# Expert rows in a fused attention and mixture-of-experts kernel: normed rows stored once and fetched by a list of row numbers

## The chip, the cores and the metric

The kernel runs as one program on the 8 cores of one Trainium2 chip. The metric is the device time in microseconds (us) of the slowest core. Cores exchange nothing; each computes 2048 of the 16384 rows of the output.

## The reference

```python
x = x + attn(layernorm(x))        # x: (2, 8192, 1024) f32
x = x + ffn(layernorm(x))

# attn: q, k, v = split(x @ W + b); softmax(q k^T / 32, causal) @ v
# ffn, for each row x of its input:
logits = x @ router_w             # 8 experts
topw, topi = top_k(softmax(logits), 2)
routed = sum over the 2 chosen experts e of topw * (silu(x @ w1[e]) @ w2[e])
gate, up = split(x @ shared_gate_up)
shared = sigmoid(x @ shared_gate_w) * ((silu(gate) * up) @ shared_down)
return routed + shared
```

## The kernel before, in words

A core owns 16 tiles of 128 rows (`NT = 16`) and works through the causal attention of its batch in 8 blocks of 1024 keys (`NKB = 8`). A unit is a pair (key block kb, row tile t); 72 units run in the order of the list `units`. Per unit TensorE (PE) makes the scores (`qk`, L542), VectorE (DVE) the row maximum, ScalarE (ACT) the exponentials `P` (L572), a transposing DMA on SP's queue turns them into `PT` (L589), and PE multiplies by the normed rows of the block (`av`, L605). The keys' rows are loaded on POOL's queue (L69), normed into `XN` on ACT (L277) and turned into `XT` by transposing DMAs on SP's queue (L287). Scores wait for all of `XT` that they read, `av` waits for `PT`.

When a tile has seen its last block it is retired in four steps that are laid between the units: `retire_a` and `retire_b` finish the attention and norm the row into `xf` (two buffers), `retire_c` makes the router's decision, `retire_d` (L739) counts each row's place in its two experts. Every expert has 640 places (`CAP = 640`), place numbers lie in `posu`. Two indirect DMAs on POOL's queue (L761) then write each row of `xf`, 2 KB in bf16, into the two places of the DRAM tensor `G`. So that places that no row takes hold zeros, 16 DMAs (L840, x = 2 to 17 of the unit loop) write zeros over the first 5120 rows of `G`, 640 KB each; they sit on POOL's queue among the loads of `xkv` rows and, from x = 10, the 8 pieces of the value weights `WV` (L845).

After attention come the shared expert's first product (`gate_up`, L790) and then the 8 experts. An expert's 640 rows are one DMA `xn<-G` (`load_rows`, L914) on SP's queue; PE turns them with the identity (`turn_rows`, L921), 8 transposes for each of 5 groups of 128 rows. Expert 0 is loaded and turned under `gate_up`. In the expert loop (L1079) expert ex does its first product (L1089, 128 matmuls of 320 columns), then its second (L1114, 5 groups s of 16 matmuls), and the turning of expert ex+1's groups lies between these groups, for s = 0 to 3. At s = 3, when expert ex+1's rows have left `xn`, the rows of expert ex+2 are loaded. `Y<-ys` (L1129, on SP's queue) stores each group of 128 result rows, 512 KB in f32, from three buffers `ys`. The weights come on POOL's queue in 8 pieces each, cast from f32 to bf16 on the way: `w1` of expert ex+2 after the first product of ex, `w2` of ex+2 after the second. Six tiles of the attention's result were parked in DRAM and come back (`O<-R`, L949, on SP's queue) after expert 0's first product.

At the end POOL gathers result rows from `Y` by `lohi`, the lower and the higher place of each row (L1150), DVE adds them (L1158), and PE's last product (L1174) adds the shared expert.

SP's and POOL's queues are in order: an instruction that waits holds back all that stand behind it. Two queues of transfers result, one for what SP issues and one for what POOL issues; both are served by the same 16 DMA engines.

Of the kernel before, what the change touches and what calls it, by code (L numbers as in the profile page):

```python
# [81 lines left out]
def build_program():  # L82
    nc = bass.Bass("TRN2", target_bir_lowering=False)

    def dram(name, shape, dty=F32, kind="ExternalInput"):
        return nc.dram_tensor(name, shape, dty, kind=kind).ap()
# [16 lines left out]
    G = dram("G", [7 * CAP + 2048, D], BF16, kind="Internal")  # L103
# [6 lines left out]
    def at(name, cols, dty, off):  # L110
        return nc.alloc_sbuf_tensor_at(name, [128, cols], dty, offset=base + off)
# [12 lines left out]
    zero = at("zero", 1024, BF16, 188416)  # L124
# [33 lines left out]
    bb_bf = at("bb_bf", 8, BF16, small_at[0] - 32)  # L158
    bqk_bf = small("bqk_bf", 16, BF16)
# [226 lines left out]
    k_tri = SP.dma(lambda e: e.dma_start(out=tri[:], in_=trih), d_tri)  # L386

# [351 lines left out]
    def retire_d(t):  # L739

        i = t % 2
        n = ring_n[0] % 3
        ring_n[0] += 1
        PE.wait(ohb_ready[t], ring_free[n], k_tri, k_ones)
        PE.quiet(lambda e: e.matmul(ring[n][:, 0:8], tri[:], ohb[i][:], start=True, stop=True))
        k = PE.do(lambda e: e.matmul(ring[n][:, 8:16], ones[:], ohb[i][:], start=True, stop=True))
        ohb_free[i] = k
        a = DVE.do(lambda e: e.tensor_tensor(out=rk[:], in0=ring[n][:, 0:8], in1=taken[:], op=ALU.add), k, k_taken[0],
                   place_tok[0])
        k_taken[0] = DVE.do(lambda e: e.tensor_tensor(out=taken[:], in0=ring[n][:, 8:16], in1=taken[:], op=ALU.add), a)  # L750
# [13 lines left out]
        xf_free[i] = [scattered[i], xf_turned[t]]  # L764
# [62 lines left out]
    while x < n_units or x <= max(retire_at):  # L827
# [11 lines left out]
        if 2 <= x < 18:  # L839
            k_zero = POOL.dma(lambda e, i=x - 2: e.dma_start(  # L840
                out=G[i * CAP // 2:(i + 1) * CAP // 2, :].rearrange("(s p) d -> p s d", p=64),
                in_=zero[0:64, :].unsqueeze(1).broadcast_to([64, CAP // 128, 1024])), d_zero, k_zeroed)
            w = slice((x - 10) * 1024, (x - 9) * 1024)
            if x >= 10:
                k_wv[0] = POOL.dma(lambda e, w=w: e.dma_start(out=WV[:, w], in_=wvh[:, w]), d_wv, proj_done[7])  # L845
# [36 lines left out]
        for fc in {70: [0, 1], 71: [2], 73: [3], 75: [4], 77: [5], 79: [6]}.get(x, []):  # L882
# [13 lines left out]
    a = DVE.do(lambda e: e.tensor_tensor(out=lohi[:, 0:NT], in0=pair(pos)[:, 0], in1=pair(pos)[:, 1], op=ALU.min),  # L896
               place_tok[0])
    k_lohi = DVE.do(lambda e: e.tensor_tensor(out=lohi[:, NT:2 * NT], in0=pair(pos)[:, 0], in1=pair(pos)[:, 1],
                                              op=ALU.max))
# [12 lines left out]

    def load_rows(queue, ex, *after):
# [17 lines left out]
    rows_in = load_rows(SP, 0, scattered[0], scattered[1], *xf_free[0], *xf_free[1], *p_free, attn_av, sg_free[0],  # L931
# [123 lines left out]

    sw, dc = call[:, 0:NT], call[:, NT:2 * NT]
# [16 lines left out]
    rows_in = load_rows(SSP, 1, rows_out)  # L1073
# [5 lines left out]
    for ex in range(8):  # L1079
# [27 lines left out]
        for s in range(CAP // 128):  # L1107
# [18 lines left out]
            else:  # L1126
# [3 lines left out]
                out=Y[ex * CAP + s * 128:ex * CAP + s * 128 + 128, :], in_=ys[q][:]), d_y[q], a)  # L1130
            if ex < 7 and s < 4:
# [6 lines left out]
                if s == 3 and ex < 6:  # L1138
                    rows_in = load_rows(SSP, ex + 2, rows_out)
# [104 lines left out]
def _prep_shared(W, b, router_w, w1, w2, sgu, sdown, sgw):  # L1244
# [41 lines left out]
```

How the kernel before makes its waits and increments, by code:

```python
    def wait(self, *tokens):  # L38
        for t in tokens:
            if t is None:
                continue
            sem, val = t
            if val <= 0 or self.passed.get(id(sem), 0) >= val:
                continue
            self.passed[id(sem)] = val
            self.q.append(lambda e, s=sem, v=val: e.wait_ge(s, v))
# [1 line left out]
    def do(self, fn, *tokens):  # L48
        self.wait(*tokens)
        self.n += 1
        self.q.append(lambda e, f=fn, s=self.sem: f(e).then_inc(s, 1))
        return (self.sem, self.n)
# [5 lines left out]
    def dma(self, fn, slot, *tokens):  # L58
        self.wait(*tokens)
        slot.n += 16
        self.q.append(lambda e, f=fn, s=slot.sem: f(e).then_inc(s, 16))
        return (slot.sem, slot.n)
# [1128 lines left out]
    def run(e, main, one, other):  # L1191
        for fn in main.q:
            fn(e)
        full = e.alloc_register("full")
        e.wait_ge(*k_flag)
        e.reg_load(full, flag[0:1, 0:1])
        with e.If_eq(full, 0):
            for fn in one.q:
                fn(e)
        with e.Else():
            for fn in other.q:
                fn(e)
```

## Time and profile before

| | us |
|---|---|
| runs shown (3): median, lowest, highest | 1340.0, 1338.53, 1341.4 |
| profiled execution, device time | 1330.74 |
| its slowest core (core 1), span | 1329.2 |
| spans of the other cores | 1301.3 to 1325.0 |
| PE busy on core 1 | 1143.0 |
| queue of POOL's DMAs, queue of SP's DMAs (share of 16 engines' span) | 45.0%, 33.8% |

The span runs from a core's first to its last instruction; the execution's own time is 1.5 us longer. An engine's busy time is an average over stages; what a wait costs is read in its own stretch. The idle time in front of an instruction, with what ended it, stands in square brackets. The time from a DMA's issue to its landing is the time until its semaphore is set.

### The profile page before, as it was taken

To read this page: it belongs to the slowest core of one execution; us is meant where nothing else is said; L and a number is where in the kernel's file an instruction comes from. 1 tells how busy PE (TensorE), PEld (TensorE's weight loads), DVE (VectorE), ACT (ScalarE), POOL (GpSimd) and SP (SyncE) were. 2 spreads that over 40 slices of the span, in tenths; PEclk is the share of its full clock that TensorE was granted. 3 is DMA by queue.
4 is the path that set the end of the run, shared out by engine and by line. 5 is a ranking of instruction groups with operands and counts; after the bars stand their busy time and mean duration, and the time that the engine had idled before them with its cause. 6 is when DMAs were issued, how large, how long until landed. Compare 5 with 4: busy or idle time off the path is not lost.

```text
span 1329.2 us, 18689 instructions; the slowest of 8 cores (1301.3 to 1329.2 us)
## 1 busy us (share of the span) xinstructions
PE 1143.0 (86%) x6280; PEld 580.2 (44%) x6280; DVE 574.2 (43%) x1273; ACT 465.8 (35%) x900; POOL 268.6 (20%) x443
## 2 busy tenths in 40 slices
PE   4778879749989898898988669699996999999987
PEld 1355545324434343343433224244553666665533
DVE  2345335425666665566676654421111111111566
ACT  2234233323543543454546444421321222222200
POOL 4101201121022111222122022260021221121531
PEclk9889889889999998899999979899998999999988
DMA  9937842994767867785969666499189999999977
GB/s 163 236 72 158 203 88 66 205 196 107 140 167 148 167 139 150 152 206 130 184 123 210 94 129 121 89 182 166 40 206 196 214 218 219 213 220 225 325 253 263
DMA packets 258956, 225.43 MB, mean 170 GB/s; under 512 B 197284, under 2 KB 203556, under 8 KB 258856
## 3 DMA queue, kind: packets, MB, share of 16 engines
q0 software_dynamic: 52976, 129.02, 45.0%
q1 hardware_dynamic: 205880, 95.14, 33.8%
q8 instruction: 54, 0.88, 0.3%
q14 instruction: 46, 0.38, 0.1%
HBM read 172.22 MB, written 51.38 MB: 168 GB/s over the span
## 4 chain that ended last, share of the span: by engine, by line
PE 51%; DMA 17%; DVE 12%; ACT 9%; issue 6%; SPq 4%; POOL 0%; DVEq 0%; ACTq 0%; POOLq 0%
PE po L605 9%; PE sp L1089 9%; PE po L1114 8%; PE sp L790 8%; PE sp L542 5%; DMA PT<-P 5%; PE po L484 4%; PE po L1174 4%; DMA XT<-XN 3%; DVE per_unit L560 3%; PE po L666 3%; ACT P L572 3%; SPq L287 2%; DMA O<-xkv 2%; DMA gb<-Y,lohi 2%
## 5 line engine op out<-in xcount | busy, mean ns | idle before, releaser
L605 PE MATMUL po<-XN,PT 128*128 128x512 bf16 x1088 | 257.7, 391 | 42.3 <-DMA PT<-P 28.2
L542 PE MATMUL sp<-XT,QT 128*128 128x512 bf16 x1088 | 252.1, 384 | 34.4 <-DMA XT<-XN 31.4
L605 PEld LDWEIGHTS po<-XN,PT 128*128 128x128 bf16 x1088 | 107.4, 100 | 183.3 <-issue 69.1
L542 PEld LDWEIGHTS sp<-XT,QT 128*128 128x128 bf16 x1088 | 105.2, 99 | 163.1 <-issue 44.5
L1127 DVE COPY ys<-po 128x1024 f32<-128x1024 f32 x35 | 42.9, 1225 | 230.7 <-PE po L1114 211.2
L790 PE MATMUL sp<-QT,WGU 128*128 128x512 bf16 x512 | 116.7, 389 | 5.2 <-DVE HB L805 5.2
L570 ACT ACTIVATE per_unit<-nm,s_q 128x1 f32<-128x1 f32 x72 | 21.2, 295 | 260.8 <-DVE nm L567 117.5
L618 DVE SCALAR_TENSOR_TENSOR O<-O,per_unit,po 128x512 f32<-128x512 f32 x112 | 80.4, 742 | 49.8 <-PE po L605 48.4
L484 PE MATMUL po<-XT,M 128*128 128x256 bf16 x512 | 67.8, 299 | 27.7 <-DMA XT<-XN 15.2
L1096 ACT ACTIVATE hT<-sp 128x640 bf16<-128x640 f32 x64 | 45.0, 703 | 113.5 <-PE sp L1089 113.5
L560 DVE TENSOR_REDUCE per_unit<-sp 128x1 f32<-128x1024 f32 (+1 forms) x72 | 83.5, 1160 | 1.6
L69 POOL DMA_DIRECT2D xs<-xkv x60 | 32.5, 546 | 244.6 <-ACT XN L277 154.0
L572 ACT ACTIVATE P<-sp,per_unit 128x1024 bf16<-128x1024 f32 (+1 forms) x72 | 76.7, 1066 | 10.5
L790 PEld LDWEIGHTS sp<-QT,WGU 128*128 128x128 bf16 x512 | 50.5, 100 | 67.7 <-issue 12.1
L666 PE MATMUL po<-WV,QT 128*128 128x512 bf16 x256 | 64.8, 399 | 11.6 <-DVE O L618 9.1
L484 PEld LDWEIGHTS po<-XT,M 128*128 128x128 bf16 x512 | 54.0, 107 | 42.3 <-issue 31.4
L1114 PE MATMUL po<-W,hT 128*128 128x512 bf16 x320 | 72.3, 379 | 0.0
L1114 PE MATMUL po<-SW,hT 128*128 128x512 bf16 x320 | 72.3, 381 | 0.0
L1089 PE MATMUL sp<-xt,W 128*128 128x320 bf16 x512 | 70.4, 299 | 1.5 <-ACT xt L926 1.5
L1089 PE MATMUL sp<-xt,SW 128*128 128x320 bf16 x512 | 70.2, 299 | 0.0
L926 ACT ACTIVATE xt<-sp 128x1024 bf16<-128x1024 bf16 x35 | 35.1, 1022 | 93.3 <-PE sp L921 93.3
L69 POOL DMA_DIRECT2D O<-xkv x64 | 34.2, 542 | 159.1 <-ACT mvr L262 81.0
(147 smaller groups left out, 1348.8 us busy)
## 6 DMA issues: line engine op xcount, KB each, us to landing
Y<-ys SPq DMA_DIRECT2D x40, 512.0 KB, 7.9
O<-xkv POOLq DMA_DIRECT2D x64, 256.0 KB, 5.3
xs<-xkv POOLq DMA_DIRECT2D x60, 256.0 KB, 4.4
G<-zero POOLq DMA_DIRECT2D x16, 640.0 KB, 8.6
xn<-G SPq DMA_DIRECT2D x8, 1280.0 KB, 20.2
xr<-xkv POOLq DMA_DIRECT2D x16, 512.0 KB, 4.8
W<-w1p POOLq DMA_DIRECT2D x32, 256.0 KB, 15.5
W<-w2p POOLq DMA_DIRECT2D x32, 256.0 KB, 20.6
```

The lines of the kernel that those rows point to most:

```text
L69: k = queue.dma(lambda e, i=i: e.dma_start(out=out[:, i * w:(i + 1) * w], in_=src[:, i * v:(i + 1) * v]), slot, *tokens)
L484: fn = lambda e, d1=d1, d2=d2, i=i: e.matmul(ring[i][:, 0:256], M[:, d1 * 1024 + d2 * 128:d1 * 1024 + d2 * 128 + 128], rhs(d1), start=(d1 ...
L542: fn = lambda e, d=d, h=h: e.matmul(sp[j][:, h * 512:h * 512 + 512], QT[:, d * 2048 + t * 128:d * 2048 + t * 128 + 128], XT[kb % 2][:, h * ...
L560: a = DVE.do(lambda e: e.reduce_max(lb[:, z:z + 1], sp[j][:, 0:n], axis=AX.X, negate=True), a)
L572: exp_tok[x] = ACT.do(lambda e: e.activation(out=P[p][:, 0:n], in_=sp[j][:, 0:n], func=AF.Exp, bias=ebias[:, z:z + 1], accum_out=lsum[:, z ...
L605: fn = lambda e, c=c, h=h, i=i: e.matmul(ring[i], PT[p][:, c * 128:c * 128 + 128], XN[kb % 2][:, c * 1024 + h * 512:c * 1024 + h * 512 + 5 ...
L618: ring_free[i] = DVE.do(lambda e, i=i, dst=dst: e.scalar_tensor_tensor(out=dst, in0=dst, scalar=corr[:, z:z + 1], in1=ring[i], op0=ALU.mul ...
L666: PE.quiet(lambda e, d=d, h=h, b=b: e.matmul(ring[b], QT[:, d * 2048 + t * 128:d * 2048 + t * 128 + 128], WV[:, d * 1024 + h * 512:d * 102 ...
L790: fn = lambda e, d=d, part=part: e.matmul(sp[j][:, part * 512:part * 512 + 512], WGU[fc][:, d * 256 + part * 128:d * 256 + part * 128 + 12 ...
L1089: fn = lambda e, d=d, h=h, fc=fc, i=i, j=j, xt_=xt_: e.matmul(sp[j][:, h * 512:h * 512 + H], SW1[i][:, d * 1024 + fc * 128:d * 1024 + fc * ...
L1114: fn = lambda e, fc=fc, h=h, s=s, i=i, j=j: e.matmul(po[j][:, h * 512:h * 512 + 512], hT[:, fc * CAP + s * 128:fc * CAP + s * 128 + 128], ...
L1174: fn = lambda e, fc=fc, h=h, j=j, t=t: e.matmul(po[j][:, h * 512:h * 512 + 512], HB[:, fc * 2048 + t * 128:fc * 2048 + t * 128 + 128], SW1 ...
```

## The change

The normed row is stored once, in order, in the DRAM tensor `F` (one plain DMA for each tile, in `retire_c`). `L` is a list of row numbers in DRAM, one 4-byte number for each place. The two indirect DMAs of `retire_d` now write the row's number (from the constant `token`) into `L`, not the row into `G`. `L` is zeroed by one small DMA on SP's queue near the start, so an empty place holds row number 0; the 16 DMAs of zeros are gone. After the last scatter, SP loads the list into `idx` (128 partitions, 5 numbers for each of 8 experts). `load_rows` becomes 5 indirect DMAs of 128 rows each, on POOL's queue for every expert. Row i of group s of an expert is now place 5p+s, so `Y` is written with a stride of 5 rows. `token` lies where `lohi` lies, so `lohi` is computed later, in the part after the branch (two DVE instructions of 16 columns). The constants `token` and the zeroed list are two more DMAs on SP's queue before its second run of transposes.

```diff
     def retire_c(t):
         i = t % 2
         PE.wait(xf_turned[t], k_rw, misc_free[0])
+        scattered[i] = POOL.dma(lambda e: e.dma_start(out=F[t * 128:(t + 1) * 128, :], in_=xf[i][:]), d_sc[i], ret[t]["xf"])
...
         for c in range(2):
             scattered[i] = POOL.dma(lambda e, c=c: e.indirect_dma_start(
-                out=G[:, :], out_offset=bass.IndirectOffsetOnAxis(ap=posu[:, 2 * t + c:2 * t + c + 1], axis=0),
-                in_=xf[i][:], in_offset=None), d_sc[i], a, ret[t]["xf"], k_zero)
+                out=L[:, :], out_offset=bass.IndirectOffsetOnAxis(ap=posu[:, 2 * t + c:2 * t + c + 1], axis=0),
+                in_=token[:, t:t + 1], in_offset=None), d_sc[i], a, k_token, k_zero)
...
-        if 2 <= x < 18:
-            k_zero = POOL.dma(lambda e, i=x - 2: e.dma_start(
-                out=G[i * CAP // 2:(i + 1) * CAP // 2, :].rearrange("(s p) d -> p s d", p=64),
-                in_=zero[0:64, :].unsqueeze(1).broadcast_to([64, CAP // 128, 1024])), d_zero, k_zeroed)
+        if 10 <= x < 18:
...
+    k_idx = SP.dma(lambda e: e.dma_start(
+        out=idx[:].rearrange("p (e i) -> p e i", e=8), in_=L[0:8 * CAP, :].rearrange("(e p i) o -> p e (i o)", e=8, p=128)),
+        d_tri, scattered[0], scattered[1], wv_done)
+
     def load_rows(queue, ex, *after):
-        return queue.dma(lambda e: e.dma_start(
-            out=xn_[:].rearrange("p (s d) -> p s d", s=5),
-            in_=G[ex * CAP:(ex + 1) * CAP, :].rearrange("(s p) d -> p s d", p=128)), d_xn, *after)
+
+        for i in range(CAP // 128):
+            c = ex * (CAP // 128) + i
+            k = queue.dma(lambda e, i=i, c=c: e.indirect_dma_start(
+                out=xn_[:, i * 1024:(i + 1) * 1024], out_offset=None, in_=F[:, :],
+                in_offset=bass.IndirectOffsetOnAxis(ap=idx[:, c:c + 1], axis=0)), d_xn, k_idx, *after)
+        return k
...
-    rows_in = load_rows(SP, 0, scattered[0], scattered[1], *xf_free[0], *xf_free[1], *p_free, attn_av, sg_free[0],
+    rows_in = load_rows(POOL, 0, scattered[0], scattered[1], *xf_free[0], *xf_free[1], *p_free, attn_av, sg_free[0],
                         sg_free[1])
...
-    rows_in = load_rows(SSP, 1, rows_out)
+    rows_in = load_rows(SPOOL, 1, rows_out)
...
-                out=Y[ex * CAP + s * 128:ex * CAP + s * 128 + 128, :], in_=ys[q][:]), d_y[q], a)
+                out=Y[ex * CAP:(ex + 1) * CAP, :].rearrange("(p i) d -> p i d", p=128)[:, s, :], in_=ys[q][:]), d_y[q], a)
...
                 if s == 3 and ex < 6:
-                    rows_in = load_rows(SSP, ex + 2, rows_out)
+                    rows_in = load_rows(SPOOL, ex + 2, rows_out)
```

What moves on POOL's queue, first in the attention's first block, where `xs` and `O` are buffers for rows of `xkv`. Before:

```order
L69 DMA O_58<-xkv 128x512 x2
L69 DMA O_57<-xkv 128x512 x2
L840 DMA G<-zero 64x5x1024 x3
L69 DMA xs_79<-xkv 128x512 x2
L840 DMA G<-zero 64x5x1024
L69 DMA xs_80<-xkv 128x512 x2
L840 DMA G<-zero 64x5x1024
L845 DMA WV<-wvh 128x1024
```

Now:

```order
L69 DMA O_58<-xkv 128x512 x2
L69 DMA O_57<-xkv 128x512 x2
L69 DMA xs_79<-xkv 128x512 x2
L69 DMA xs_80<-xkv 128x512 x2
L849 DMA WV<-wvh 128x1024 x2
L69 DMA xs_79<-xkv 128x512 x2
```

The zero DMAs are gone and the order of the rest is kept. Second, POOL's queue at the turn to the experts, where W is `W1` or `W2` and SW the second buffer of each. Before:

```order
L69 DMA W_141<-w1p 128x1024 x8
L69 DMA W_143<-w2p 128x1024 x8
L1196 TENSOR_LOAD flag
L1197 COMPARE_AND_BRANCH
L69 DMA SW_165<-w1p 128x1024 x8
L69 DMA SW_166<-w2p 128x1024 x8
L69 DMA W_141<-w1p 128x1024 x8
L69 DMA W_143<-w2p 128x1024 x8
```

Now:

```order
L69 DMA W_142<-w1p 128x1024 x8
L69 DMA W_144<-w2p 128x1024 x8
L922 DMA xn<-F,idx 128x1024 x5
L1209 TENSOR_LOAD flag
L1210 COMPARE_AND_BRANCH
L69 DMA SW_167<-w1p 128x1024 x8
L69 DMA SW_168<-w2p 128x1024 x8
L922 DMA xn<-F,idx 128x1024 x5
L69 DMA W_142<-w1p 128x1024 x8
L922 DMA xn<-F,idx 128x1024 x5
L69 DMA W_144<-w2p 128x1024 x8
```

The fetches of an expert's rows stand between the weights' loads: that of expert ex+2 behind `w1` of ex+2 and ahead of `w2` of ex+2. Before they stood on SP's queue between the stores of `Y`:

```order
L1129 DMA Y<-ys_162 128x1024
L1129 DMA Y<-ys_163 128x1024
L914 DMA xn<-G 128x5x1024
L1129 DMA Y<-ys_164 128x1024
L1129 DMA Y<-ys_162 128x1024
```

On SP's queue now only the stores are left there.

## Rows read from the trace of the kernel before

**Rows 1.** Cores: span and mean granted TensorE clock of each.

```profile
core 1: 1329.2 us, clock 0.942
...
core 6: 1325.0 us, clock 0.945
```

**Rows 2.** Waits of PE on core 1: us in total, times, longest us.

```profile
PE sp L542 <- DMA XT<-XN: 31.4, 5, 14.0
PE po L605 <- DMA PT<-P: 28.2, 10, 5.8
...
PE sp L921 <- DMA xn<-G: 12.2, 1, 12.2
```

**Rows 3.** PE in order of time, 244 to 306 us: start, us, instructions, [idle before].

```profile
246.66 5.21 PE L605 MATMUL po<-XN,PT 128*128 128x512 bf16 x16 [5.82 <-DMA PT<-P]
...
279.19 3.61 PE L605 MATMUL po<-XN,PT 128*128 128x512 bf16 x16 [3.52 <-DMA PT<-P]
...
298.51 3.57 PE L542 MATMUL sp<-XT,QT 128*128 128x512 bf16 x8 [13.98 <-DMA XT<-XN]
```

**Rows 4.** DMAs, 240 to 300 us: queue's packets, MB; issues, KB each, median landing.

```profile
q0 software_dynamic: 2741, 7.97, 58.4%
...
G<-zero POOLq DMA_DIRECT2D x6, 640.0 KB, 10.9
...
XT<-XN SPq DMA_TRANSPOSE x7, 8.6
PT<-P SPq DMA_TRANSPOSE x6, 6.6
```

**Rows 5.** DMA issues of the whole page: the transposes, number and median us to landing.

```profile
XT<-XN SPq DMA_TRANSPOSE x78, 4.2
PT<-P SPq DMA_TRANSPOSE x72, 4.0
```

**Rows 6.** Chain that ended last, between 270 and 300 us.

```profile
277.30 21.07 DMA XT<-XN
```

**Rows 7.** Stretches of core 1: PE, PEld, DVE, ACT, POOL busy, PEclk, DMA share, GB/s.

```profile
240.00:270.00 30.00, 22.99 (x99) 9.81 (x98) 12.53 (x24) 10.23 (x22) 7.01 (x12) 0.89 1.14 192
270.00:300.00 30.00, 12.49 (x55) 5.19 (x53) 5.79 (x10) 6.14 (x15) 4.88 (x8) 0.79 1.13 192
...
1054.00:1073.00 19.00, 19.00 (x120) 9.86 (x118) 4.90 (x4) 5.21 (x6) 4.23 (x8) 1.00 1.07 215
```

**Rows 8.** PE in order of time around expert 1's second product.

```profile
981.31 0.61 PE L921 MATMUL sp<-ident,xn 128*128 128x128 bf16 x8
...
1018.41 1.87 PE L921 MATMUL sp<-ident,xn 128*128 128x128 bf16 x16 [12.20 <-DMA xn<-G]
1020.07 4.24 PE L1114 MATMUL po<-SW,hT 128*128 128x512 bf16 x16
...
1056.69 1.06 PE L921 MATMUL sp<-ident,xn 128*128 128x128 bf16 x16
```

**Rows 9.** SP's and POOL's queues in order of time, 960 to 1040 us.

```profile
966.42 4.23 POOL L69 DMA_DIRECT2D W<-w1p  x8 [78.95 <-PE sp L1089]
...
994.83 0.39 SPq L914 DMA_DIRECT2D xn<-G  x1
...
1034.00 0.39 SPq L914 DMA_DIRECT2D xn<-G  x1
```

**Rows 10.** DMAs issued 990 to 1010 us: KB each, median us to landing.

```profile
SW<-w1p POOLq DMA_DIRECT2D x8, 256.0 KB, 23.9
...
xn<-G SPq DMA_DIRECT2D x1, 1280.0 KB, 23.4
```

**Rows 11.** POOL's indirect DMAs, the scatters to G and the gathers from Y.

```profile
L761 POOL DMA_INDIRECT G<-xf,posu x32: 956/1000/1025, 368.5 to 867.4; - x32
L1150 POOL DMA_INDIRECT gb<-Y,lohi x32: 932/938/1974, 1229.4 to 1309.2; - x32
```

**Rows 12.** Expert 0's rows: DMAs issued 860 to 890 us, and their first use on PE.

```profile
xn<-G SPq DMA_DIRECT2D x1, 1280.0 KB, 18.6
930.43 0.61 PE L921 MATMUL po<-ident,xn 128*128 128x128 bf16 x8
```

More of the change, by code:

```diff
@@ L102, in build_program @@
     trih = dram("trih", [128, 128], BF16)
-    G = dram("G", [7 * CAP + 2048, D], BF16, kind="Internal")
+    tokh = dram("tokh", [128, NT], U32)
+    F = dram("F", [NT * 128, D], BF16, kind="Internal")
+    L = dram("L", [7 * CAP + 2048, 1], U32, kind="Internal")
     R = dram("R", [6 * 128, D], kind="Internal")
@@ L123, in build_program @@
     PT = [at(f"PT{i}", 1024, BF16, 202752 + 2048 * i) for i in range(NPT)]
-    zero = at("zero", 1024, BF16, 188416)
+    zero = at("zero", 8 * CAP // 128, F32, 188416)
     mask = at("mask", 512, BF16, 206848)
@@ L158, in build_program @@
     bb_bf = at("bb_bf", 8, BF16, small_at[0] - 32)
+    token = at("token", NT, U32, small_at[0] - 128)
     bqk_bf = small("bqk_bf", 16, BF16)
@@ L386, in build_program @@
     k_tri = SP.dma(lambda e: e.dma_start(out=tri[:], in_=trih), d_tri)
+    k_token = SP.dma(lambda e: e.dma_start(out=token[:], in_=tokh), d_const[8], k_bb)
+    k_zero = SP.dma(lambda e: e.dma_start(out=L[0:8 * CAP, :].rearrange("(p i) o -> p (i o)", p=128),
+                                          in_=zero[:].bitcast(U32)), d_zero, k_zeroed)
     def evict_m(h, b, tok):
@@ L838, in build_program @@
             step(t)
-        if 2 <= x < 18:
-            k_zero = POOL.dma(lambda e, i=x - 2: e.dma_start(
-                out=G[i * CAP // 2:(i + 1) * CAP // 2, :].rearrange("(s p) d -> p s d", p=64),
-                in_=zero[0:64, :].unsqueeze(1).broadcast_to([64, CAP // 128, 1024])), d_zero, k_zeroed)
+        if 10 <= x < 18:
             w = slice((x - 10) * 1024, (x - 9) * 1024)
-            if x >= 10:
-                k_wv[0] = POOL.dma(lambda e, w=w: e.dma_start(out=WV[:, w], in_=wvh[:, w]), d_wv, proj_done[7])
+            k_wv[0] = POOL.dma(lambda e, w=w: e.dma_start(out=WV[:, w], in_=wvh[:, w]), d_wv, proj_done[7])
         if x == 18:
@@ L895, in build_program @@
     pair = lambda v: v[:].rearrange("p (t c) -> p c t", c=2)
[L896 to L899, printed above, removed]
     w1_ready, w2_ready = {}, {}
@@ L911, in build_program @@
     bank_bf = [b[:].bitcast(BF16) for b in bank]
+    idx = at("idx", 8 * CAP // 128, U32, 209152)
+    k_idx = SP.dma(lambda e: e.dma_start(
+        out=idx[:].rearrange("p (e i) -> p e i", e=8), in_=L[0:8 * CAP, :].rearrange("(e p i) o -> p e (i o)", e=8, p=128)),
+        d_tri, scattered[0], scattered[1], wv_done)
     def load_rows(queue, ex, *after):
-        return queue.dma(lambda e: e.dma_start(
-            out=xn_[:].rearrange("p (s d) -> p s d", s=5),
-            in_=G[ex * CAP:(ex + 1) * CAP, :].rearrange("(s p) d -> p s d", p=128)), d_xn, *after)
+        for i in range(CAP // 128):
[4 more added lines that the diff above has]
+        return k
     def turn_rows(pe, act, s_, b, dst, *after):
@@ L1054, in build_program @@
     H = CAP // 2
+    a = SDVE.do(lambda e: e.tensor_tensor(out=lohi[:, 0:NT], in0=pair(pos)[:, 0], in1=pair(pos)[:, 1], op=ALU.min),
+               place_tok[0], scattered[0], scattered[1])
+    k_lohi = SDVE.do(lambda e: e.tensor_tensor(out=lohi[:, NT:2 * NT], in0=pair(pos)[:, 0], in1=pair(pos)[:, 1],
+                                              op=ALU.max))
     sw, dc = call[:, 0:NT], call[:, NT:2 * NT]
@@ L1257, in _prep_shared @@
     trih = np.triu(np.ones((128, 128), np.float32), 1)
+    tokh = np.ascontiguousarray(np.arange(2048, dtype=np.uint32).reshape(16, 128).T)
     iotah = np.ascontiguousarray(np.broadcast_to(np.arange(8, dtype=np.float32), (128, 8)))
     return dict(wqt=wqt, wkt=wkt, wvh=wvh, bqk=bqk, bvh=bvh, rwgh=rwgh, w1p=w1p, w2p=w2p, wguh=wguh,
-                dwh=rows(f(sdown)), iotah=iotah, trih=trih, idenh=np.eye(128, dtype=np.float32))
+                dwh=rows(f(sdown)), iotah=iotah, trih=trih, tokh=tokh, idenh=np.eye(128, dtype=np.float32))
 def kernel(L0_attn_x, L0_attn_W, L0_attn_b, L0_ffn_router_w, L0_ffn_w1, L0_ffn_w2,
```

## The prediction

> **What bounds the kernel now.** The spans of the cores come first [rows 1]: core 1 sets the time with 1329.2 us. The profiled execution took 1330.74 us, 9.3 us under the median of the three runs (1340.0); the sum below is made against the profiled one and then taken off the median. PE is the busiest engine, so the second view is what PE waits for, longest first [rows 2]. Three of its waits touch this change: for the turned keys `XT` (31.4 us), for the turned exponentials `PT` (28.2 us) and for an expert's rows `xn` (12.2 us, one wait).
>
> Third, where they lie. PE in order of time [rows 3] shows 5.82 us for `PT` at 246.66, 3.52 us for `PT` at 279.19 and 13.98 us for `XT` at 298.51. The stretches [rows 7] give the sum: from 240 to 300 us PE is busy 22.99 + 12.49 of 60 us, so 24.5 us idle. All of it stands behind DMAs, and the DMA share there is full (1.14 and 1.13). The DMAs issued in that time [rows 4] say with what: POOL's queue moved 7.97 MB, and the 6 DMAs of zeros among them are 6 x 640 KB, 3.9 MB, close to half. The transposes, on the other queue but the same engines, landed after 8.6 and 6.6 us in the median against 4.2 and 4.0 over the whole run [rows 5]; the last one took 21.07 us and is a step of the chain that ended last [rows 6].
>
> Fourth, expert 1's second product [rows 8]. The rows of expert 1 have left `xn` at 981.9 us (981.31 + 0.61). The load of expert 2's rows is issued at 994.83 [rows 9], 12.9 us later: on SP's queue it stands behind stores of `Y` whose buffers are not yet free. It lands after 23.4 us [rows 10], and PE, ready at 1006.2 (1018.41 less 12.20), waits to 1018.4. In the later rounds there is no such wait: issue at 1034.00 [rows 9], use at 1056.69 [rows 8], 22.7 us apart. But the DMA share of that stage is 1.07 with PE never idle [rows 7]: both are full.
>
> **The zeros.** Sixteen DMAs of 640 KB go. Their issues on POOL cost nothing on the path. What they cost is the transposes' time. Taking half of POOL's bytes out of the crowded 60 us should halve the extra time of the transposes: the idle 24.5 us become 12.2, gain 12.2. The bounds are 4 us (the transposes are late for their own issue on SP's queue, and the weights `WV` and rows of `xkv` still fill the DMA engines) and 24.5 us (all of it goes). I take the middle since the share of zeros is near one half [rows 4]. After each stall PE also runs at its lower level of 1.2 GHz for a while: the granted clock is 0.89 and 0.79 [rows 7], 16 matmuls took 5.21 us instead of the 3.61 of an undisturbed group, and 8 took 3.57 instead of about 1.8 [rows 3]. These two are 3.4 us; with those after the 279 us wait I call it 4.6, and half comes back: 2.3, bounds 0 and 4.6. Together **-14.5**.
>
> **The scatters.** Before, 32 indirect DMAs of 256 KB at 1.0 us of POOL each [rows 11]. Now 16 plain stores of 256 KB and 32 indirect ones of 512 bytes. POOL gets 16 more issues; nothing on the path waits for POOL there, since the new store waits only for `xf`, which the scatter waited for as well, three units earlier in the loop. 4 MB less traffic over 500 us: I count **0**, bounds +3 (POOL later with loads of keys) and -3 (transposes a little quicker). The Trainium skill, "DMA: Bandwidth & Descriptors", section "Specifications", speaks against this part: a transfer under 512 B is done as a read and a write. By it each number would cost twice its packet. No row here shows a store that small to DRAM; if the page held and each pair of scatters were as slow as the 256 KB ones, the sum would not change, as nothing reads the list before the last scatter.
>
> **The list, and expert 0's rows.** The old load was issued at about the end of the scatters and landed after 18.6 us; its first use is at 930.43 [rows 12]. Now the list comes first. It is 1024 pieces of 20 bytes. I bound it by a transpose from below (4.2 us, [rows 5]) and by the slowest transpose beside full weight loads from above (21.07 us, [rows 6]). Then 5 gathers are issued, at the price of a gather from `Y`: 0.94 us and a gap, taken as the scatters' 1.0 plus 0.27, so 6.3 us [rows 11]. From 873 us the worst case is 873 + 21 + 6.3 + 18.6 = 919 us, before 930.4. Cost **0**; the cover is `gate_up`, and without it some 40 us would stand open. Behind the waiting gathers on POOL stand only weights of expert 1, first used behind the second product in [rows 8]. `lohi`'s two small DVE instructions move to a place where DVE idles: 0. Two more SP issues near the start: 0, bound +1.
>
> **The gathers in the expert loop.** Expert 2's are no longer behind the stores of `Y`: issued from 981.9 instead of 994.8. They need 6.3 us of issue, and on their queue they stand behind `w1` of expert 2. With the old landing time of 23.4 us the last lands at 981.9 + 6.3 + 23.4 = 1011.6 at worst, and at 1005.4 if the issue is hidden. I take a rest of 1 us of the 12.2, and 1.4 us of slow clock with it (1.87 us for 16 transposes against 1.06, 4.24 against 3.62, [rows 8]): gain 12.6, bounds 7 and 13.6. The later five rounds pay some of it back. PE is now 12 us earlier against DMA engines that were already full [rows 7], and the fetch waits behind `w1`, whose pieces landed after 23.9 us in the median [rows 10] and were issued 15.5 us before the rows would be (966.42 [rows 9] to 981.9). I put 1.2 us on each of five rounds, 6 us, bounds 0 and 12.6 (all of it). Together **-6.6**.
>
> The rule that speaks against this part is in the Trainium skill, "SBUF — State Buffer", section "Who interferes with whom": VectorE in a 2-port mode holds the port pair that GpSimd needs to write descriptors, and GpSimd waits for the whole instruction. By it a gather issued on POOL could cost up to one DVE instruction more; if that were as much again in each round as the 1.2 us set above, the sum would be -15, not -21. The trace does not bear it out: the 32 gathers from `Y`, issued while DVE adds, took 0.938 us in the median, the least 0.932 [rows 11].
>
> **Sum.** -14.5 - 6.6 = -21 us: 1330.7 becomes 1309.6, and the median 1340 becomes 1319. Core 6 is 4 us behind core 1 [rows 1] and has the same waits, so the slowest core stays near this.
>
> **The rivals.**
>
> A, *the expert stage gives all back*. The DMA engines bound it and the 12.6 us return as waits for rows or for the last gathers from `Y`. For it: the share of 1.07. Against: weights are issued a whole round ahead. Then only -14.5: 1325.5.
>
> B, *everything goes*. All 24.5 and 4.6 us of the attention's stall and 13.6 of the experts': -43, 1297. Against: `WV` and keys still crowd the engines at 270 us.
>
> C, *the transposes are late for another reason*, SP's own queue, and the experts give back: no change, 1340. For it: SP issues each transpose only after ACT is done. Against: 21.07 us from issue to landing is not issue time.
>
> D, *slower: the rows stand behind the weights*. On POOL's queue a fetch can't pass `w1` of 4 MB, while on SP's queue it shared the engines with it. The landing then becomes the issue's 6.3 us plus the 23.9 us of the weights' pieces [rows 10], 30.2 us against the 22.7 us that a round gives: 7.5 us late, in 6 rounds 45 us, against 28 us gained: +17, 1357. It decides from 4.7 us per round. Against it: `w1` has a head start of 15.5 us.
>
> **How the numbers follow.** The forecast has 0.50, A 0.22, B 0.11, C 0.07, D 0.10. Only a difference over 0.2% (2.7 us) can be told from no change. Faster are the forecast, A and B, and a share of C: 0.85; same 0.05; slower 0.10. The forecast's own range is 1308 to 1331. The range asked for reaches up through A with the attention term at its lower bound of 4 us (1336), and down into B, to 1302.
>
> **What would show it.** Right: no G or zeros, XT's last landing in the first block about 11 us, PE idle between 240 and 300 us about 12 us, no wait of 12 us for `xn` but several of 1 to 2 us, expert 0's rows there before PE wants them. Wrong: transposes still landing after 15 us or more there; waits of 5 us and more for `xn` in each round; or a wait of PE at the first `turn_rows`.

## The result, and the profile after

| | before | after |
|---|---|---|
| median (lowest to highest), us | 1339.26 (1335.96 to 1341.4) | 1374.37 (1360.82 to 1388.02) |
| profiled execution, us | 1330.74 | 1360.82 |
| its slowest core, span us | core 1, 1329.2 | core 7, 1359.0 |

The ratio is 1.0229, with a 95% interval of 1.0164 to 1.0295: the change makes the kernel slower by some 30 us. (It counts only executions in the faster of two states of the chip, and so lies below the quotient of the medians.) The forecast said 21 us faster. The profiled execution is the quickest of the four, so what follows is the low end of the loss.

The spans of the changed kernel show first that no single core is odd; compare [rows 1].

```profile
core 0: 1320.4 us, clock 0.949
core 1: 1351.5 us, clock 0.941
...
core 3: 1349.9 us, clock 0.932
...
core 5: 1352.0 us, clock 0.933
...
core 7: 1359.0 us, clock 0.933
```

To see where the time went, each core's span is cut at three marks: the first matmul with `WV` (the end of the first block), the last `av` matmul, and the first product with expert 0's `w1`. Means over the 8 cores of the profiled executions:

| stretch, us | before | after | difference |
|---|---|---|---|
| start to first `WV` matmul | 323.3 | 308.6 | -14.7 |
| first `WV` matmul to last `av` | 475.3 | 497.0 | +21.7 |
| last `av` to first product with `w1` | 139.3 | 141.5 | +2.2 |
| from there to the end (the experts' stage) | 378.0 | 394.7 | +16.7 |
| span | 1315.9 | 1341.8 | +25.9 |

The first row is the forecast's term for the zeros, almost to the microsecond. Two stretches for which the forecast had 0 and -6.6 cost 38 us together. The waits of PE on core 7 of the changed kernel (line, what it waited for: us in total, times, longest) name the transfers, and the same core of the kernel before stands below it:

```profile
PE po L612 <- DMA PT<-P: 45.1, 14, 12.1
PE sp L549 <- DMA XT<-XN: 27.8, 5, 8.9
PE sp L930 <- DMA xn<-F,idx: 21.5, 4, 7.4
```

```profile
PE sp L542 <- DMA XT<-XN: 25.9, 4, 8.3
PE po L605 <- DMA PT<-P: 24.7, 9, 5.6
PE sp L921 <- DMA xn<-G: 9.7, 2, 9.5
```

Over all cores the waits for `PT` rose from 25.1 us in the mean to 32.0, those for `xn` from 8.6 to 19.0. These are sums over the whole span, and the first block, where waits fell, hides part of the rise. Between the first `WV` matmul and the last `av` alone, the waits for `PT` rose from 13.8 to 26.2 us and those for `XT` from 18.1 to 24.0, and PE's busy time rose from 416.3 to 422.6 us with the granted clock down from 0.956 to 0.939. In the experts' stage PE idles 11.2 us more (25.6 before, 36.8 now), nearly all of it for `xn`, and is busy 5.5 us longer (352.4 and 357.9) with the clock at 0.957 instead of 0.972. So about a third of each loss is not a wait but matmuls at a lower granted clock.

**The first block.** PE of core 7 in order of time, answering to [rows 3]:

```profile
269.54 3.61 PE L612 MATMUL po<-XN,PT 128*128 128x512 bf16 x16 [2.34 <-DMA PT<-P]
...
279.66 3.57 PE L549 MATMUL sp<-XT,QT 128*128 128x512 bf16 x8 [4.78 <-DMA XT<-XN]
...
298.50 3.61 PE L612 MATMUL po<-XN,PT 128*128 128x512 bf16 x16 [1.95 <-DMA PT<-P]
```

In this stretch no wait over 5 us is left. (The wait of 13.98 us in [rows 3] was on core 1; core 7 had 6.54 us at that place before.) The time from issue to landing of `XT<-XN` between 240 and 300 us, and the stretches that answer to [rows 7] (columns: busy us and count of PE, PEld, DVE, ACT and POOL, granted clock, DMA share, GB/s), on the same core:

```profile
DMA to landing us min/median/max: 3.2/5.1/11.3
```

```profile
240.00:270.00 30.00, 27.66 (x130) 12.40 (x128) 15.51 (x30) 15.03 (x32) 7.53 (x14) 1.00 0.95 173
270.00:300.00 30.00, 23.27 (x94) 9.63 (x93) 11.92 (x21) 6.58 (x16) 2.68 (x5) 0.89 0.67 122
```

PE of core 7 idles 9.1 us there (60 less 27.66 and 23.27); over the cores the idle time of these 60 us fell from 18.8 to 7.9 us.

**The attention after it.** Here the new loss lies. Three stretches of core 7, the changed kernel first:

```profile
350.00:400.00 50.00, 41.13 (x199) 17.83 (x198) 27.27 (x78) 20.10 (x48) 10.57 (x16) 0.97 1.02 124
400.00:450.00 50.00, 33.49 (x134) 13.39 (x132) 22.06 (x63) 12.53 (x32) 9.46 (x14) 0.80 0.75 120
700.00:750.00 50.00, 31.25 (x127) 12.96 (x126) 21.83 (x45) 20.29 (x39) 8.81 (x15) 0.81 1.14 149
```

The kernel before, same core:

```profile
350.00:400.00 50.00, 43.16 (x205) 18.77 (x203) 30.27 (x91) 22.05 (x51) 9.00 (x13) 0.93 0.70 151
400.00:450.00 50.00, 45.98 (x230) 20.61 (x229) 31.05 (x90) 21.98 (x52) 10.46 (x16) 1.00 0.75 164
700.00:750.00 50.00, 43.09 (x199) 18.67 (x196) 31.80 (x70) 27.30 (x57) 5.32 (x10) 0.97 0.78 158
```

At 350 us the DMA share rises from 0.70 to 1.02 while the bytes fall from 151 to 124 GB/s: the engines are occupied and move less. The trace's single packets say how. Between 300 and 880 us the packets that last over 1.5 us take, summed and divided by the 16 engines, 14.9 us before and 57.8 us after (means of the cores; the longest 3.8 and 8.3 us). They lie in bursts in the microseconds after the scatters into `L`: 28.9 of the 57.8 us belong to packets that start within 8 us after a scatter, where the kernel before, after its scatters into `G`, has 0.8. It is not the scatters' own packets that are long (those of 32 bytes, 8 numbers each, take 15 ns in the mean on core 7) but whatever moves then: rows of `xkv`, transposes, and the parking of `O`, whose landing time in the changed kernel

```profile
R<-O POOLq DMA_DIRECT2D x6, 512.0 KB, 11.8
```

was 5.7 us before.

**The list and expert 0's rows** cost nothing, as forecast. The list lands 20.8 us after its issue on core 7, but 23.3 to 26.2 us on four of the others, over the bound of 21.07 [rows 6] that the prediction had set; the cover holds all the same. POOL stands for 21.27 us until it can issue the first gather, and the gathers' landing is quick. First the first gather in order of time, then what the trace says of the five (duration of the instruction, landing):

```profile
917.66 1.01 POOL L922 DMA_INDIRECT xn<-F,idx  x1 [21.27 <-issue]
```

```profile
L922 POOL DMA_INDIRECT xn<-F,idx x5: 942/948/1008, 917.7 to 922.6; - x5
...
DMA to landing us min/median/max: 7.2/7.7/18.7
```

PE turns these rows at 946.7 us without a wait.

**The expert loop.** PE of core 7, the waits for rows, where [rows 8] had a single one of 12.20 us:

```profile
1028.45 1.87 PE L930 MATMUL sp<-ident,xn 128*128 128x128 bf16 x16 [5.94 <-DMA xn<-F,idx]
...
1075.11 1.87 PE L930 MATMUL sp<-ident,xn 128*128 128x128 bf16 x16 [7.36 <-DMA xn<-F,idx]
...
1153.30 1.05 PE L930 MATMUL sp<-ident,xn 128*128 128x128 bf16 x16 [1.44 <-DMA xn<-F,idx]
...
1197.08 1.86 PE L930 MATMUL sp<-ident,xn 128*128 128x128 bf16 x16 [6.73 <-DMA xn<-F,idx]
```

Three waits over 5 us; the prediction had named such waits "in each round" as a sign that it is wrong. Here they come in three of six rounds, and on every core in at least one.

### The profile page after: what moved, and what is told of

The parts are those of the page before. It is cut to its first block, busy times and chain, and to the rows that moved or that the text cites. A ratio compares the mean times of both kernels' runs of the same rounds, so it can differ in the third digit from the quotient of the medians.

```text
span 1359.0 us, 18727 instructions; the slowest of 8 cores (1320.4 to 1359.0 us)
## 1 busy us (share of the span) xinstructions
PE 1154.3 (85%) x6280; PEld 583.7 (43%) x6280; DVE 573.9 (42%) x1273; ACT 466.2 (34%) x900; POOL 304.5 (22%) x483
## 4 chain that ended last, share of the span: by engine, by line
PE 46%; DMA 22%; DVE 10%; ACT 7%; issue 7%; SPq 5%; POOL 1%; DVEq 0%; ACTq 0%; POOLq 0%
PE po L612 9%; PE po L1127 7%; DMA xn<-F,idx 7%; PE sp L798 7%; PE sp L549 6%; PE sp L1102 5%; DMA PT<-P 4%; PE po L491 4%; PE po L1187 4%; DMA XT<-XN 3%; SPq L290 3%; PE po L673 3%; DVE per_unit L567 2%; DMA O<-xkv 2%; ACT P L579 2%
## 5 line engine op out<-in xcount | busy, mean ns | idle before, releaser
L612 PE MATMUL po<-XN,PT 128*128 128x512 bf16 x1088 | 264.3, 398 | 59.9 <-DMA PT<-P 45.1
L922 POOL DMA_INDIRECT xn<-F,idx x40 | 38.7, 967 | 160.2 <-PE sp L930 86.4
```

Source lines behind the costliest of these rows:

```text
L612: fn = lambda e, c=c, h=h, i=i: e.matmul(ring[i], PT[p][:, c * 128:c * 128 + 128], XN[kb % 2][:, c * 1024 + h * 512:c * 1024 + h * 512 + 5 ...
```

## The experiments

Two questions: what makes the attention 22 us longer, and what makes the experts 17 us longer. The stages in the table are means over the cores of one profiled execution each; single cores differ by up to 23 us from that mean. The kernels ran on several chips, each beside the kernel before on the same chip, and the ratios are against that one. How far a mean moves by chance can be read from kernels that do the same work in a stage: the first stage, with the zeros where they were, took 323.3 to 331.3 us (before, e2, e3, e5, e6), and the experts' stage with the old loads 377.8 to 380.9.

| kernel | to first `WV` | `WV` to last `av` | experts' stage | PE waits `PT` / `xn` | ratio to before, 95% |
|---|---|---|---|---|---|
| before | 323.3 | 475.3 | 378.0 | 25.1 / 8.6 | |
| after | 308.6 | 497.0 | 394.7 | 32.0 / 19.0 | 1.0229, 1.0164 to 1.0295 |
| e1_zero_early | 324.2 | 473.8 | 380.9 | 16.6 / 7.2 | 0.9961, 0.9839 to 1.0083 |
| e2_list4 | 331.3 | 519.3 | 380.1 | 54.1 / 9.4 | 1.0273, 1.0178 to 1.0368 |
| e3_list512 | 327.3 | 476.7 | 378.9 | 19.5 / 8.4 | 0.9970, 0.9889 to 1.0051 |
| e5_list64 | 324.9 | 472.4 | 377.9 | 19.7 / 7.8 | 1.0005, 0.9973 to 1.0038 |
| e6_list4wide | 328.6 | 470.2 | 377.8 | 19.7 / 8.1 | one execution, 1338.94 us |
| e4_constlist | 305.8 | 471.9 | 380.4 | 12.8 / 7.2 | 0.9756, 0.9667 to 0.9846 |
| e9_spread4 | 306.6 | 493.5 | 378.4 | 30.5 / 4.8 | 1.0082, 1.0040 to 1.0124 |
| e8_rows64 | 309.1 | 466.4 | 385.2 | 10.6 / 6.4 | 0.9807, 0.9752 to 0.9863 |
| e10_rows64_row0 | 312.5 | 468.3 | 402.8 | 12.1 / 20.6 | 0.9934, 0.9888 to 0.9979 |
| e11_rows16 | 311.2 | 478.0 | 382.5 | 15.2 / 8.4 | 0.9875, 0.9820 to 0.9929 |
| e12_plain_sp | 308.4 | 468.0 | 382.1 | 11.5 / 9.9 | 0.9752, 0.9689 to 0.9815 |
| e13_rows64_again | 307.7 | 467.0 | 385.0 | 10.9 / 4.0 | 0.9783, 0.9719 to 0.9847 |

### Are the zeros dear only where they lie?

e1_zero_early is the kernel before with all 16 DMAs of zeros moved into x = 2 to 9, away from the crowded end of the block:

```diff
-        if 2 <= x < 18:
-            k_zero = POOL.dma(lambda e, i=x - 2: e.dma_start(
+        if 2 <= x < 10:
+            for i in (2 * x - 4, 2 * x - 3):
+                k_zero = POOL.dma(lambda e, i=i: e.dma_start(
```

> The kernel before, with all 16 DMAs of zeros issued in units 2 to 9 of the first key block, two for each unit, so that none lies beside the turning of the second block's keys. Everything else stays. Theory Z (the zeros cost time because they share the DMA engines with the transposes at 240 to 300 us): most of the 14.7 us that the changed kernel gained before its first retired tile comes back, 8 to 14 us faster, PE's idle time between 240 and 300 us about 10 us instead of 24. Rival (the transposes are late for their own issue, and the changed kernel gained by something else): no change within 3 us.

It came out at 1341.92 us against 1350.58 for the kernel before beside it, which the interval can tell neither from no change nor from the expected 8 to 14 us. The stages say more. PE's idle time between 240 and 300 us did fall as expected, to 6.1 us in the mean from 18.8. But the last matmul of the projections moved from 219.5 to 237.8 us, and the first `WV` matmul stayed at 324.2: what the block's end gained, its middle lost. Against the 323 to 331 us of the kernels with the zeros in their old place, moving them is worth between nothing and 7 us; leaving them out gives 305.8 to 312.5. So most of the price of the 10 MB of zeros was paid in both places that were tried.

### Is it the scatters, and is it their size?

To the kernel before, which keeps its zeros, its scatters into `G` and its loads, 32 further scatters are added with the same row numbers and a table `L` that nobody reads. Only the width of one row of `L` differs: 4 bytes, 64 bytes, 512 bytes.

```diff
                 in_=xf[i][:], in_offset=None), d_sc[i], a, ret[t]["xf"], k_zero)
+            scattered[i] = POOL.dma(lambda e, c=c: e.indirect_dma_start(
+                out=L[:, :], out_offset=bass.IndirectOffsetOnAxis(ap=posu[:, 2 * t + c:2 * t + c + 1], axis=0),
+                in_=xf[i][:, 0:2], in_offset=None), d_sc[i])
```

(for e3_list512 `0:256`, for e5_list64 `0:32`.)

> The kernel before, plus 32 indirect DMAs that write 4 bytes for each of 128 rows into a list nothing reads, behind the scatter of the rows. Theory S (the 4-byte scatter is what the changed kernel lost by between its first retired tile and the experts, 20 to 40 us on the slow cores): 15 to 40 us slower, and after each pair of them one transfer on each of the 16 DMA engines lasts several us. Rival P (the loss is from the plain store of the row or from POOL's queue being later): at most 5 us slower.

> As the kernel with the extra 4-byte scatters, but each row writes 512 bytes into a list whose rows are 512 bytes. If it is the small size of a write (or several writes into one stretch of memory) that stalls the engines: at most 4 us slower than before. If it is the extra indirect DMA as such: as slow as with 4 bytes.

> The kernel before plus 32 indirect DMAs that write 64 bytes for each row into a list with rows of 64 bytes. 4 bytes cost 2.7%, 512 bytes nothing. If the price is for a write that shares its 64 bytes of memory with others or covers them only in part: no loss, at most 0.5%. If it is for every write under 512 bytes: a loss of the order of 2 to 3%, as with 4 bytes.

With 4 bytes the kernel is 2.7% slower and the stage 44 us longer (519.3 against 475.3, or against the 476.7 of e3_list512 on the same chip); with 64 and with 512 bytes it is as long as before. All three issue the same 32 instructions on POOL, so neither the issues nor the number of packets is the cost. It is the write of 4 bytes. The packets over 1.5 us take 49.1 us of the engines with 4 bytes (14.9 before), 12.9 with 64, and in this stage PE waits 46.9 us for `PT` (13.8 before), 8.9 with 64 bytes. Core 7 of e2_list4 and of e5_list64:

```profile
PE po L606 <- DMA PT<-P: 40.9, 11, 13.8
PE po L606 <- DMA PT<-P: 19.5, 11, 6.3
```

Why the stage loses more than in the changed kernel, which scatters just as many numbers, stays open. The Trainium skill, "DMA: Bandwidth & Descriptors", section "Specifications", has its border at 512 bytes; if that alone had set the price, 64 bytes would have been as dear as 4, and they were not.

e6_list4wide keeps the 4 bytes but multiplies the place by 64, so that neighbouring places lie 256 bytes apart:

```diff
+    L = dram("L", [(7 * CAP + 2048) * 64, 2], BF16, kind="Internal")
...
+        aw = DVE.do(lambda e: e.tensor_scalar(out=posw[:, 2 * t:2 * t + 2], in0=pos[:, 2 * t:2 * t + 2], scalar1=64.0,
+                                              scalar2=None, op0=ALU.mult), b)
...
+                out=L[:, :], out_offset=bass.IndirectOffsetOnAxis(ap=posw[:, 2 * t + c:2 * t + c + 1], axis=0),
```

> The kernel before plus 32 indirect DMAs of 4 bytes for each row, but the 4 bytes of neighbouring places lie 256 bytes apart. Theory N (neighbouring places are written by several DMA engines at about the same time into one stretch of memory, and these writes wait for each other): the long transfers after the scatters go, first retired tile to last scores within 5 us of the kernel before (476 to 482 us). Theory S (each write of 4 bytes is dear by itself): that stage is as long as with the dense list (517 to 525 us).

1338.94 us and a stage of 470.2 us: nothing is lost, in one execution, with packets over 1.5 us taking 16.4 us. A small write far from the others is cheap; many small ones to neighbouring places at about the same time are dear. The 128 numbers of one scatter go to 8 experts, and those of one expert to places close together; in the dense list they lie within a few tens of bytes of each other. That their writes meet there is argued from this, not seen.

### What slows the experts?

e4_constlist is the changed kernel without the scatters into `L`. The list is a constant in which every entry, the empty places' too, names another row.

```diff
-        for c in range(2):
-            scattered[i] = POOL.dma(lambda e, c=c: e.indirect_dma_start(
-                out=L[:, :], out_offset=bass.IndirectOffsetOnAxis(ap=posu[:, 2 * t + c:2 * t + c + 1], axis=0),
-                in_=token[:, t:t + 1], in_offset=None), d_sc[i], a, k_token, k_zero)
...
+        tokh=tokh, listh=(np.arange(8 * CAP) * 29 % 2048)
```

> The changed kernel without the 32 scatters of row numbers; the list is a constant of the host that names 5120 rows spread over F, so the gathers have the same number and size but fetch other rows (the output's expert part is not the reference's). Theory S: the stage from the first retired tile to the experts is as long as in the kernel before, and the 14.7 us gained ahead of it are kept; the experts' stage keeps what it loses in the changed kernel (9 to 24 us by core): 1330 to 1345 us in all. Rival P: within 5 us of the changed kernel's 1361 to 1376 us. If the experts' stage also recovers (to some 370 us on the slowest core), its loss came from the rows that the true list names, 8 x 100 or so empty places that all fetch row 0.

Both losses vanish: the attention's stage is 471.9 us, the experts' 380.4, the time 1315.89, where 1330 to 1345 had been expected with the experts' loss still in it. That the gathers stand behind the weights on POOL's queue is as true here as in the changed kernel, so rival D's mechanism can't be what cost 17 us. Two causes were left: the list written by scatters, or what it says. e9_spread4 keeps the 4-byte scatters and changes only the default with which `L` is filled, from 0 to spread row numbers:

```diff
-    k_zero = SP.dma(lambda e: e.dma_start(out=L[0:8 * CAP, :].rearrange("(p i) o -> p (i o)", p=128),
-                                          in_=zero[:].bitcast(U32)), d_zero, k_zeroed)
+    k_zero = SP.dma(lambda e: e.dma_start(out=L[0:8 * CAP, :].rearrange("(p i) o -> p (i o)", p=128), in_=dflt), d_zero)
```

> The changed kernel with one edit: the list's default names rows spread over F, not row 0. The 4-byte scatters stay. Theory H (the empty places' fetches of the one row 0 slow the experts' stage, from 381 to 395 us in the mean): experts' stage back to 375 to 385 us, about 14 us faster than the changed kernel. Rival (the stage is slower since the true rows are fetched out of order, or for another reason): no change.

The experts' stage falls to 378.4 us and the waits for `xn` to 4.8, while the attention's stage stays long (493.5): the two losses are separate. 4096 of the 5120 places are taken; the other 1024, a fifth, hold 0 in the changed kernel, and all of them fetch row 0 of `F`.

### The version without either loss

e8_rows64 is the changed kernel with list rows of 64 bytes (16 copies of the number) and a spread default. SP loads the wide list, one POOL instruction takes its first column. (The constant `token` is loaded later too, at x = 4, as it now takes twice the room.)

```diff
-    L = dram("L", [7 * CAP + 2048, 1], U32, kind="Internal")
+    L = dram("L", [7 * CAP + 2048, 16], U32, kind="Internal")
...
-                in_=token[:, t:t + 1], in_offset=None), d_sc[i], a, k_token, k_zero)
+                in_=token[:, t:t + 16], in_offset=None), d_sc[i], a, k_token, k_zero)
...
+    k_idx = POOL.do(lambda e: e.tensor_copy(idx[:], wide_[:].rearrange("p (c o) -> p c o", o=16)[:, :, 0]), k_idx)
```

> The changed kernel with list rows of 64 bytes (the scatter writes the number and 15 columns behind it), a default list that names rows spread over F in place of zeros, and POOL taking column 0 of each list row out. If a 64-byte write is cheap and the experts' stage suffers from empty places that all fetch row 0: near the kernel with the constant list, 1316 to 1325 us, 1.5 to 2.4% faster than before. If 64 bytes are as dear as 4: 1345 to 1360 us.

1315.45 us, 1.9% under the kernel before (0.9807) and some 4% under the changed one. Run again as e13_rows64_again it gave 1315.95 (0.9783).

> The kernel of 1315 us once more, unchanged, beside the one with plain loads on the same chip: 1310 to 1320 us, experts' stage 378 to 390 us, sum of waits for xn under 11 us on every core. If it comes out over 1325 us, the first reading was a lucky chip.

The time and the waits for `xn` (4.0 us in the mean) came as expected. The experts' stage did in its mean, 385.0 us, but that is made of 372.0 to 382.1 us on six cores and of 403.8 and 407.9 us on cores 6 and 7 (see the last section).

e10_rows64_row0 puts only the default 0 back:

```diff
-    dflt = np.ascontiguousarray(np.repeat((np.arange(8 * CAP) * 29 % 2048).astype(np.uint32), 16).reshape(128, 640))
+    dflt = np.ascontiguousarray(np.repeat((np.arange(8 * CAP) * 0).astype(np.uint32), 16).reshape(128, 640))
```

> The changed kernel with list rows of 64 bytes, as the kernel of 1315 us, but the list's default entries all name row 0 again, as in the change. Theory H (the empty places of every expert fetch one row, and that slows the experts' stage whatever the scatters do): stage from the first product with w1 to the end 12 to 18 us longer than the 378 to 405 us of the spread list, waits for xn of 15 us and more in all, time 1328 to 1334 us; the attention's stage stays at 460 to 480 us. Rival (the two effects are one: the fetches were slow only because list entries of 4 bytes had been written by many engines): 1313 to 1319 us, waits for xn under 11 us.

1333.23 us: the experts' stage is 17.6 us longer again and the waits for `xn` are back at 20.6 us in the mean, with the attention's stage untouched at 468.3. Part of both means is the late ACT of the last section; on cores 0 to 3, which have none of it in either kernel, the stage took 395.9 us against 382.1, so by this pair the shared row costs 14 to 18 us. PE of core 6 of this kernel:

```profile
982.73 1.20 PE L933 MATMUL sp<-ident,xn 128*128 128x128 bf16 x16 [4.22 <-DMA xn<-F,idx]
...
1028.59 1.87 PE L933 MATMUL sp<-ident,xn 128*128 128x128 bf16 x16 [7.13 <-DMA xn<-F,idx]
```

The packets show it without a wait's attribution. The gathers' packets are of 4 KB on POOL's queue; from 960 to 1200 us one of them takes 307 ns in the mean in the changed kernel and 310 in e10_rows64_row0, but 223 in e8_rows64 and 229 in e9_spread4, while those of 2 KB beside them take 218 to 222 ns in all four. Half of the 4 KB packets take no more than 159 ns in each of the four; what differs is how many are late: 14% last over 600 ns with the shared row, 5 to 6% without. Many fetches of one row at a time are slower than as many of different rows.

How far apart must the entries lie? e11_rows16 is e8_rows64 with rows of 16 bytes:

```diff
-    L = dram("L", [7 * CAP + 2048, 16], U32, kind="Internal")
+    L = dram("L", [7 * CAP + 2048, 4], U32, kind="Internal")
```

> The kernel of 1315 us with list rows of 16 bytes in place of 64. Theory (writes collide when neighbouring places share a stretch of memory of 64 bytes; with 16 bytes a row four places share one, with 4 bytes sixteen): the stalls come back in part, the stage from the first product with WV to the last av 475 to 495 us, time 1320 to 1335 us. Rival (rows of 16 bytes are wide enough, or the count of sharers does not matter down to four): 460 to 480 us, time 1313 to 1319 us. A third outcome, as bad as 4 bytes (484 to 511 us, about 1340 us), would say that any sharing is enough.

The stage is 478.0 us against 466.4 with 64 bytes and 493.5 with 4 (e9_spread4), the long packets take 22.1 us against 13.2 and 50.0, and the time is 1325.18 us, inside the 1320 to 1335 of the theory, though its interval overlaps that of e8_rows64. The cost grows as the places move closer. That places which share a stretch of memory hinder each other fits this; the size of such a stretch was not found (64 bytes is the smallest spacing seen to be free).

### What are the gathers' queue and place worth?

Last, the term of -6.6. e12_plain_sp is e8_rows64 with the rows of experts 1 to 7 loaded as in the kernel before, by one plain DMA on SP's queue:

```diff
+        return queue.dma(lambda e: e.dma_start(
+            out=xn_[:].rearrange("p (s d) -> p s d", s=5),
+            in_=F[ex * 192:ex * 192 + CAP, :].rearrange("(s p) d -> p s d", p=128)), d_xp, *after)
...
-                    rows_in = load_rows(SPOOL, ex + 2, rows_out)
+                    rows_in = load_rows(SSP, ex + 2, rows_out)
```

> The kernel of 1315 us, but the rows of experts 1 to 7 are fetched as before: one plain DMA of 640 rows on SP's queue behind the stores of Y, here from F at fixed rows. It leaves out which rows an expert gets: experts 1 to 7 work on rows that the list does not name, in the same number. Theory of the prediction (gathers on POOL's queue, issued 13 us earlier, are worth 6.6 us): a wait for xn of 10 us or more in expert 1's second product is back, the experts' stage 5 to 9 us longer than with gathers (mean 385 us there), time 1320 to 1325 us. Rival A (the DMA engines bound that stage, so it gives all back): the wait for xn is back, but the stage is as long within 3 us, time 1312 to 1319 us. Rival G (gathers themselves cost, by POOL's issues or by their 2 KB pieces in list order): the stage is 4 us or more shorter than with gathers, time under 1312 us.

The old wait is back, on core 0 for instance:

```profile
987.00 1.87 PE L938 MATMUL sp<-ident,xn 128*128 128x128 bf16 x16 [12.28 <-DMA xn<-F]
```

but the experts' stage is 382.1 us, against 385.0 with gathers beside it (378.1 without the two odd cores), and the time 1310.5 us against 1315.95, with intervals that overlap widely. The stage fits rival A (within 3 us); the time lies below the 1312 to 1319 that A expected, where rival G (gathers cost by themselves) had put it, but G's 4 us in the stage are not there, so these runs don't decide between the two. What they speak against is the forecast's view, 1320 to 1325 us without the gathers: PE loses 4.0 us for `xn` with them instead of 9.9 without, and the end comes no earlier.

## Why the prediction was wrong

**The zeros, -14.5: right in sign and size, the closeness partly luck.** Measured -14.7 at the first `WV` matmul. On core 1 the idle time from 240 to 300 us fell from 24.5 to 6.2 us, further than the 12.2 of the prediction, and the last `XT` landed after 11.3 us on core 7 where about 11 was foreseen. The half was taken of POOL's 7.97 MB alone; of all that moved in these 60 us (11.54 MB on core 1) the zeros were a third, and the idle time fell by three quarters. The argument from place was too narrow as well: the term was built on the crowded 60 us, and e1_zero_early shows the zeros costing most of the same when they lie before them.

**The scatters, 0 with bounds +3 and -3: the step that failed.** Measured +21.7. The step asked who waits for a scatter, and its answer holds: "nothing reads the list before the last scatter". It did not ask what a scatter does to the 16 engines while the transposes `PT` and `XT` need them, and those are the waits that grew, by 12.4 and 5.9 us in this stage. The Trainium skill's rule on transfers under 512 bytes was looked up and then set aside for the same wrong reason, that only the scatters' own end would be late. It is to the rule's credit that it pointed at the right instructions. Its border and its price are not what the runs show: the extra cost was nil for 64 bytes and for spaced 4 bytes, and dear for dense ones. The lower bound of -3 may have been too tight as well: with harmless scatters in place of the old ones the stage fell from 475.3 to 466.4 and 467.0 us. The kernels that still write each row twice without loss lie between 470.2 and 476.7, and e4_constlist, without any scatter, at 471.9; so what writing each row once is worth, some 3 to 10 us, is not known closely.

**The list and expert 0's rows, 0: right.** The cover of `gate_up` held. What is left of the +2.2 us there was not followed up.

**The gathers in the expert loop, -6.6: measured +16.7**, by a cause that the prediction doesn't contain. It priced a gather by the count of rows and by the instruction; the front part said that an empty place holds row number 0, and the step never followed that sentence into the transfers. Without the shared row the term is 0 within about 4 us (378.4 in e9_spread4 against 378.0 before; e12_plain_sp against e13_rows64_again). What PE gains at expert 2 is paid back elsewhere in the stage, as in rival A; that it goes to DMA engines that were full is argued, not shown. The 0.948 us of a gather on POOL was priced right: the gathers of the loop took 948 ns in the median as those under `gate_up` did, 1012 at most. That neither bears out nor refutes the rule that the prediction took from the Trainium skill, "SBUF — State Buffer", section "Who interferes with whom", since no row shows a DVE instruction in that mode beside them. The prediction's own row settled no more, and it left out that one of the 32 gathers from `Y` took 1974 ns [rows 11].

**Rival D** had the right sign, the right symptom (waits over 5 us) and the wrong mechanism: e4_constlist and e9_spread4 keep the fetch behind the weights and lose the long waits. The 30 us lost are two mechanisms that no rival held. That e8_rows64, which has neither, came out at 1315.5 us near the forecast of 1319 is luck: its attention's stage is 9 us shorter than before where the forecast had 0, and its experts' stage 7 us longer where the forecast had 6.6 less.

## What to carry to other kernels

A transfer that nobody waits for is not free: cost it by what it does to the engines that it shares with transfers on the path, and take the DMA share together with GB/s (1.02 at 124 GB/s against 0.70 at 151 was a stall, not traffic). Give a list that is scattered into DRAM entries 64 bytes apart, the smallest spacing that cost nothing here, or test a smaller one. And the default of an index list is an access pattern: spread it, for a fifth of all fetches going to one row cost 14 to 18 us here, as much as leaving out the zeros had saved.

## What the runs showed of the hardware

- **Neighbouring 4-byte writes stall all engines.** 32 scatters of 128 numbers made the packets over 1.5 us take 49 to 58 us of all 16 engines instead of 15, half of it within 8 us after a scatter, the longest packet 8.3 us in the changed kernel. 16 bytes a row: 22 us. 64 bytes, 512 bytes or 4 bytes at a spacing of 256: 13 to 16 us, as without them. That the writes collide in one stretch of memory fits all of these; the mechanism inside the memory was not seen.
- **One row fetched by many is slow**: 307 to 310 ns in the mean for a packet of 4 KB against 223 to 229 with spread rows, by more late packets (14% over 600 ns against 5 to 6%) at the same median of 159. The Trainium skill, "DMA: Bandwidth & Descriptors", section "Latency and other measured facts", reports a loss of rate when the 128 rows of a copy lie at certain wide distances from each other; no run here varied the distance, and whether a shared row is the same effect is open.
- **A wait that stays open.** On cores 6 and 7 of e13_rows64_again and core 7 of e8_rows64 the experts' stage took 23 to 30 us more than on the others. There ACT starts a pair of `Silu` late, on core 7 of e13_rows64_again in every first product, released by something that the trace calls remote. Every profiled kernel has such late starts on two to four of its cores, mostly of cores 4 to 7, the kernel before too (10.9 us on its core 7); only in e8_rows64, e10_rows64_row0 and e13_rows64_again do they add up to 20 us and more on a core. Core 7 of e13_rows64_again, ACT in order of time:

```profile
1123.30 1.30 ACT L1112 ACTIVATE hT<-sp 128x640 bf16<-128x640 f32 x2 [8.27 <-remote]
...
1164.32 1.30 ACT L1112 ACTIVATE hT<-sp 128x640 bf16<-128x640 f32 x2 [8.35 <-remote]
...
1232.13 1.30 ACT L1112 ACTIVATE hT<-sp 128x640 bf16<-128x640 f32 x2 [21.85 <-remote]
```

PE of that core stands for some 2.5 us in the middle of each first product and for 20.22 us in the last. It is no wait for `xn` (these cores have none), its cause was not looked for by an experiment, and these cores set the time of the profiled executions of this version.
